# First expert layer of a four-layer tower: three float32r products of split operands for each float32 product

## What is computed

```python
logits = xf @ gate_w + gate_b
probs = jax.nn.softmax(logits, axis=-1)
gates, expert_idx = jax.lax.top_k(probs, K)          # K = 2 of E = 8
h = jax.nn.relu(jnp.einsum('nc,ech->neh', xf, w1) + b1)      # 256 -> 512
expert_out = jnp.einsum('neh,ehc->nec', h, w2) + b2          # 512 -> 256
...
out = jnp.einsum('ne,nec->nc', weights, expert_out)
return out.reshape(b, t, c)
```

## Time and profile before

| | |
|---|---|
| time, median of 3 runs | 1462.86 us (1462.44 to 1463.99) |
| the profiled execution | 1469.06 us, its span 1467.1 us |
| mean granted TensorE clock | 0.907 of full |
| TensorE busy | 1262.5 us (86% of the span) |
| VectorE busy | 956.9 us (65%) |
| GpSimd busy | 712.7 us (49%) |
| ScalarE busy | 528.6 us (36%) |
| first mixture, first to last product | 531.7 to 826.9 us |
| its tiles | 71 |

### The profile page before, as it was taken

The page is one execution under the profiler, slowest core; times in us unless marked ns, Lnnn a source line. Parts: engine busy times, 40 slices in busy tenths (PEclk is TensorE's granted clock), DMA queues, the critical chain, the costliest instruction groups (busy, mean ns, idle before and its releaser), DMA issues. The chain is left out here.

```text
span 1467.1 us, 23655 instructions
## 1 busy us (share of the span) xinstructions
PE 1262.5 (86%) x6856; PEld 891.6 (61%) x6856; DVE 956.9 (65%) x2759; ACT 528.6 (36%) x999; POOL 712.7 (49%) x912
## 2 busy tenths in 40 slices
PE   1358989989999759999999658899995899999997
PEld 0245656656666436666666447777774567667675
DVE  6657989988887455555555578999985444444443
ACT  1025545546565412222222266666652111111111
POOL 6664286282222244445555246666663454544543
PEclk9869989989999769999999868887887899999999
DMA  6266646546874513211211242321000821101000
GB/s 175 49 103 111 116 79 133 84 84 141 168 149 108 200 47 107 72 63 62 65 60 53 80 143 94 103 90 48 22 16 30 295 98 32 33 29 32 27 18 12
DMA packets 88714, 125.79 MB, mean 86 GB/s; under 512 B 17728, under 2 KB 71630, under 8 KB 87632
## 3 DMA queue, kind: packets, MB, share of 16 engines
q1 hardware_dynamic: 68800, 84.61, 25.2%
q0 software_dynamic: 16416, 38.46, 8.4%
q10 hardware_dynamic: 3376, 1.22, 0.4%
HBM read 70.71 MB, written 31.01 MB: 69 GB/s over the span
## 5 line engine op out<-in xcount | busy, mean ns | idle before, releaser
L1064 DVE TENSOR_REDUCE top_a_a<-s_bank 128x4 f32<-128x1024 f32 x128 | 156.2, 1220 | 60.0 <-PE s_bank L704 54.9
L883 ACT ACTIVATE prob_a<-s_bank 128x1024 f32<-128x1024 f32 x128 | 130.6, 1020 | 42.1 <-PE s_bank L725 39.5
L2025 PE MATMUL ebank<-w,exT 128*128 x312 | 142.7, 601 | 0.7 <-ACT exT L2071 0.7
L2036 PE MATMUL ebank<-w,ehT 128*128 x624 | 141.2, 379 | 0.9 <-ACT ehT L2079 0.9
L1582 PE MATMUL mbank<-w2T_m,fhT_m 128*128 128x256 f32 x512 | 140.6, 437 | 0.0
L615 POOL DMA_INDIRECT rows_d<-h_a,row_i_a x64 | 64.6, 1009 | 152.9 <-DVE row_i_a L1149 138.2
L1262 PE MATMUL ebank<-w,exT 128*128 x284 | 135.5, 600 | 0.6 <-ACT exT L1309 0.6
L1274 PE MATMUL ebank<-w,ehT 128*128 x568 | 134.5, 380 | 0.8 <-ACT ehT L1315 0.8
L1219 POOL DMA_INDIRECT ex<-rows_d,tile_row x71 | 72.3, 1019 | 123.8 <-DVE ey L1347 108.7
L1582 PEld LDWEIGHTS mbank<-w2T_m,fhT_m 128*128 128x128 f32 x512 | 117.2, 229 | 22.3
L2036 PEld LDWEIGHTS ebank<-w,ehT 128*128 128x128 f32 x624 | 115.6, 190 | 15.7 <-issue 1.6
(11 more groups left out here) (350 smaller groups left out, 2696.3 us busy)
## 6 DMA issues: line engine op xcount, KB each, us to landing
w<-in_L_ffn_W SPq DMA_DIRECT2D x16, 1024.0 KB, 10.3
qs_a<-parts_q_a SPq DMA_DIRECT2D x96, 128.0 KB, 4.4
ks_a<-parts_k_a SPq DMA_DIRECT2D x96, 128.0 KB, 4.6
w<-in_L_ffn_w SPq DMA_DIRECT2D x16, 512.0 KB, 5.9
image_a<-in_x SPq DMA_DIRECT2D x4, 1024.0 KB, 8.3
ya_m<-y_d SPq DMA_DIRECT2D x16, 256.0 KB, 2.8
yb_m<-y_d SPq DMA_DIRECT2D x16, 256.0 KB, 3.1
b<-in_L_ffn_b SPq DMA_DIRECT2D x8, 512.0 KB, 9.4
```

What stands on the lines that cost most here:

```text
L883: nc.scalar.activation(prob[:, j % 4].rearrange("p g t s -> p (g t s)"), s2_bank[:].rearrange("p g s -> p (g s)"), ACT.Exp, scale=HD ** -0 ...
L1064: nc.vector.tensor_reduce(top[:, j].rearrange("p g t -> p (g t)"), s1_bank[:].rearrange("p g (t s) -> p (g t) s", t=TPI), axis=AX, op=ALU. ...
L2025: last = nc.tensor.matmul(bank[1 + n % 2][:], xT[j % 2][:, ch, :], w[:, bass.ds(e, 1), at:at + 512].rearrange("p a f -> p (a f)"), start=c ...
L2036: last = nc.tensor.matmul(bank[4 + j % 2][:, 0:D], hT[j % 2][:, f, :], w[:, bass.ds(e, 1), at:at + D].rearrange("p a d -> p (a d)"), start ...
```

## The change

It touches `experts`, and the SBUF layout of its neighbours.

- Each weight and each stationary operand is split into a float32r part (rounded) and a low part (the remainder, float32r too). Each float32 product becomes three float32r products: high by high, high by low, low by high (`three`).
- Operands: ScalarE's copies to `xT` and `hT` round to float32r; VectorE subtracts for the low parts, `xl` and `hl`.
- Weights: for expert 0 ScalarE copies two halves to `wl`, VectorE subtracts (between the two halves of `maps`), ScalarE writes the rounded weights back into `w`. For experts 1 to 7 this goes in 28 pieces of 512: ScalarE `near`, GpSimd `low_of`, ScalarE `far`, one piece per tile. TensorE waits for `split_ok` of the tile's expert, with a value computed from the register.
- The second product runs two tiles behind instead of one, and hT has three buffers instead of two.
- The scaling of x into y moves from VectorE to ScalarE (`scaled`).
- The low weights lie in the upper half of the large zone; the fixed weights of `middle` move behind the biases, and tiles of `attention` and `middle` change places. TensorE no longer waits for all weights at the start of the stage.

```diff
@@ tower
+        low0 = zone0["high"]("w0_low", [P, E, 2 * F0 + F0 // P * D], F32R)
         zone_m = zones("_m")
-        sb = zone_m["high"]
+        sb = zone_m["above"]
...
@@ maps
-    def maps(first_done, all_done):
+    def maps(first_done, all_done, between=None):
         common()
         build(0, EARLY)
         c.eng.sem_inc(first_done, 1)
+        if between:
+            between()
         build(EARLY, count)
...
@@ experts
-    xT = [sb(f"exT{u}", [P, 2, P]) for u in range(2)]
+    HTR = 3
+    xT, xTl = ([sb(f"{n}{u}", [P, 2, P], F32R) for u in range(2)] for n in ("exT", "exTl"))
...
-    hT = [sb(f"ehT{u}", [P, FC, P]) for u in range(2)]
+    hT, hTl = ([sb(f"{n}{u}", [P, FC, P], F32R) for u in range(HTR)] for n in ("ehT", "ehTl"))
+    PIECE = 512
+    PIECES = [(e, at) for e in range(1, E) for at in range(0, 2 * width + D * FC, PIECE)]
+    PER = (2 * width + D * FC) // PIECE
...
+    def rounded(e, at, n):
+        return w[:, e, at:at + n].bitcast(F32R)
+
+    def three(pe, to, high, low, e, at, n, first, last):
+        whole = w[:, bass.ds(e, 1), at:at + n].rearrange("p a f -> p (a f)").bitcast(F32R)
+        rest = wl[:, bass.ds(e, 1), at:at + n].rearrange("p a f -> p (a f)")
+        nc.tensor.matmul(to, high, whole, start=first, stop=False)
+        nc.tensor.matmul(to, high, rest, start=False, stop=False)
+        return nc.tensor.matmul(to, low, whole, start=False, stop=last)
...
@@ gpsimd
+            c.run(nc.gpsimd.memset(nought[:], 0.0))
             pool.wait_ge(c.sem, c.n)
+            pool.sem_inc(nought_ok, 1)
...
                 if j >= XR:
                     pool.wait_ge(xT_ps, j - XR + 1)
-                    pool.wait_ge(own_ok, j - XR + 1)
+                    pool.wait_ge(scaled_ok, j - XR + 1)
...
+            def low_of(n):
+                e, at = PIECES[n]
+                pool.wait_ge(near_ok, n + 1)
+                nc.gpsimd.tensor_tensor(wl[:, e, at:at + PIECE], w[:, e, at:at + PIECE], wl[:, e, at:at + PIECE].bitcast(F32), ALU.subtract)\
+                    .then_inc(low_ok, 1)
+
             for j in range(count + XR + 1):
                 if j < count:
                     load(j)
                 if j >= XR + 1:
                     send(j - XR - 1)
+                if 2 <= j < 2 + len(PIECES):
+                    low_of(j - 2)
...
@@ tensor
-            for e in range(E):
-                pe.wait_ge(w_in[e], 32)
...
                 e = number[j]
-                pe.wait_ge(xT_ok, j + 1)
+                pe.wait_ge(split_ok, e + 1)
+                pe.wait_ge(xl_ok, j + 1)
...
                 for ch in range(2):
-                    last = nc.tensor.matmul(bank[1 + j % 2][:], xT[j % 2][:, ch, :],
-                                            w[:, bass.ds(e, 1), width * ch:width * (ch + 1)].rearrange("p a f -> p (a f)"),
-                                            start=ch == 0, stop=ch == 1)
+                    last = three(pe, bank[1 + j % 2][:], xT[j % 2][:, ch, :], xTl[j % 2][:, ch, :], e, width * ch, width, ch == 0, ch == 1)
...
                 for f in range(FC):
...
+                    last = three(pe, bank[4 + j % 2][:, 0:D], hT[j % HTR][:, f, :], hTl[j % HTR][:, f, :], e, 2 * width + D * f, D, f == 0, f == FC - 1)
...
-            for j in range(count + 1):
+            for j in range(count + 2):
                 if j < count:
                     g1(j)
                 if j + 1 < count:
                     expert_of(j + 1)
                     x2(j + 1)
-                if j >= 1:
-                    g2(j - 1)
+                if j >= 2:
+                    g2(j - 2)
                 if j < count:
                     th(j)
...
@@ scalar
+            def scaled(j):
+                u = j % YR
+                act.wait_ge(own_ok, j + 1)
+                nc.scalar.activation(y[u][:], x[j % XR][:, 0:D], ACT.Identity, bias=nought[:, 0:1], scale=own[u][:, 2:3]).then_inc(scaled_ok, 1)
+
+            def near(n):
+                e, at = PIECES[n]
+                if n % PER == 0:
+                    act.wait_ge(w_in[e], 32)
+                nc.scalar.activation(wl[:, e, at:at + PIECE], w[:, e, at:at + PIECE], ACT.Copy).then_inc(near_ok, 1)
+
+            def far(n):
+                e, at = PIECES[n]
+                act.wait_ge(low_ok, n + 1)
+                nc.scalar.activation(rounded(e, at, PIECE), w[:, e, at:at + PIECE], ACT.Copy).then_inc(far_ok, 1)
+                if n % PER == PER - 1:
+                    act.wait_ge(far_ok, n + 1)
+                    act.sem_inc(split_ok, 1)
+
+            act.wait_ge(w_in[0], 32)
+            half = PER * PIECE // 2
+            for at in (0, half):
+                nc.scalar.activation(wl[:, 0, at:at + half], w[:, 0, at:at + half], ACT.Copy).then_inc(near0_ok, 1)
+            for k, at in enumerate((0, half)):
+                act.wait_ge(low0_ok, k + 1)
+                nc.scalar.activation(rounded(0, at, half), w[:, 0, at:at + half], ACT.Copy).then_inc(far0_ok, 1)
+            act.wait_ge(far0_ok, 2)
+            act.sem_inc(split_ok, 1)
...
+            near(0)
+            near(1)
             x2(0)
             for j in range(count):
                 if j + 1 < count:
                     x2(j + 1)
                 th(j)
+                scaled(j)
+                if j + 2 < len(PIECES):
+                    near(j + 2)
+                if 1 <= j < 1 + len(PIECES):
+                    far(j - 1)
...
@@ vector
-            maps(maps_ok, all_maps)
+            def low_of_first():
+                half = PER * PIECE // 2
+                for k, at in enumerate((0, half)):
+                    dve.wait_ge(near0_ok, k + 1)
+                    nc.vector.tensor_tensor(wl[:, 0, at:at + half], w[:, 0, at:at + half], wl[:, 0, at:at + half].bitcast(F32), ALU.subtract)\
+                        .then_inc(low0_ok, 1)
+
+            maps(maps_ok, all_maps, low_of_first)
...
-                c.run(nc.vector.tensor_tensor(sent_to[u][:], own[u][:, 1:2], outside[:, j:j + 1], ALU.max))
-                nc.vector.tensor_scalar(y[u][:], tail[:, 0:D], own[u][:, 2:3], None, ALU.mult).then_inc(own_ok, 1)
+                nc.vector.tensor_tensor(sent_to[u][:], own[u][:, 1:2], outside[:, j:j + 1], ALU.max).then_inc(own_ok, 1)
...
+            def xl(j):
+                dve.wait_ge(xT_ok, j + 1)
+                nc.vector.tensor_tensor(xTl[j % 2][:].rearrange("p c s -> p (c s)"), bank[3 * (j % 2)][:, 0:2 * P],
+                                        xT[j % 2][:].rearrange("p c s -> p (c s)").bitcast(F32), ALU.subtract).then_inc(xl_ok, 1)
+
+            def hl(j):
+                dve.wait_ge(hT_ok, j + 1)
+                nc.vector.scalar_tensor_tensor(out=hTl[j % HTR][:].rearrange("p c s -> p (c s)"), in0=bank[6 + j % 2][:], scalar=0.0,
+                                               in1=hT[j % HTR][:].rearrange("p c s -> p (c s)").bitcast(F32), op0=ALU.max, op1=ALU.subtract)\
+                    .then_inc(hl_ok, 1)
...
-            for j in range(count + 1):
+            xl(0)
+            for j in range(count + 2):
                 if j < count:
                     g1(j)
+                if j + 1 < count:
+                    xl(j + 1)
+                if j < count:
                     owner(j)
-                if j >= 1:
-                    g2(j - 1)
+                if j >= 2:
+                    g2(j - 2)
+                if j < count:
+                    hl(j)
...
```

More of the change, by code:

```diff
@@ L116, in zones @@
                 "bias": Space(nc, bias, BIAS_BYTES, stage), "rest": Space(nc, rest, fixed - rest, stage),
-                "open": Space(nc, bias, fixed - bias, stage), "free": Space(nc, bias + BIAS_BYTES // 4, fixed - bias - BIAS_BYTES // 4, stage)}
+                "open": Space(nc, bias, fixed - bias, stage),
+                "above": Space(nc, bias + 4 * E * (F0 + D), BIAS_BYTES - 4 * E * (F0 + D), stage)}
     with ctx:
@@ L182, in tower @@
                              lane, tile_no, ones8, sends0, minus_half)
-            experts(nc, block, s, ctx, used, zone0, weights0, bias0, load_fixed, rows0_d, y0_d, cnt, ident, iota8, lane, tile_no, ones8)
+            experts(nc, block, s, ctx, used, zone0, weights0, low0, bias0, load_fixed, rows0_d, y0_d, cnt, ident, iota8, lane, tile_no, ones8)
             ctx0.close()
@@ L266, in attention @@
         sb = zone["high"]
-        h1 = [sb(f"h1_{u}", [P, TPI, ROW0]) for u in range(2)]
-        row_i = [sb(f"row_i{u}", [P, TPI, 2], I32) for u in range(2)]
         prob = sb("prob", [P, 4, 2, TPI, SEQ])
@@ L274, in attention @@
         res = sb("res", [P, TPI, D])
+        h1 = [sb(f"h1_{u}", [P, TPI, ROW0]) for u in range(2)]
+        row_i = [sb(f"row_i{u}", [P, TPI, 2], I32) for u in range(2)]
         sb = zone["open"]
@@ L1158, in attention, with experts @@
     return sem.all
-def experts(nc, block, s, ctx, used, zone, w, b, load_fixed, rows_d, y_d, cnt, ident, iota8, lane, tile_no, ones8):
```

(32 more changed lines are left out.)

2 lines of the change are left out of this document (1 added, 1 removed).

## The result

The changed kernel took 1453.31 us (median of 6 runs, 1450.18 to 1456.67) beside 1463.07 us (6 runs) for the kernel before: a ratio of 0.9915, with a 95% interval from 0.9888 to 0.9941. It is faster by about 10 us, where 35 were forecast. The profiled execution has a span of 1450.1 us, 17.0 less than that of before.

What follows compares the result with a forecast made beforehand. GpSimd was to bound the first 28 tiles at 3.85 us, then TensorE with its sequencer at 3.5: 10.5 us gained by tile 29, 24.6 over the last 41 tiles, tail nothing; 1462.86 - 35.1 = 1427.7 us, range 1412 to 1446.

Steps and rivals of the forecast that it cites:

- GpSimd, the bound of the first 28 tiles: First expert layer: GpSimd's load, send and added subtraction set the pace at 3.85 us per tile, ends 3.5 and 4.1.
- port rival: low_of holds chosen, sent_to or ey on VectorE in 28 tiles, up to 1.0 us each: 28 us, 1456; chance 0.07.
- GpSimd's sum: GpSimd's iteration in the first 28 tiles: 1.02 + 0.31 + 1.02 + 0.02 + 1.26 + 0.20 = 3.83, taken as 3.85 us.
- TensorE at 3.50: Expert tiles where nothing else binds: array 3.36 and sequencer 3.45 to 3.5, taken as 3.5 us against 4.10 before.
- The sequencer's term: TensorE's address steps for products with weights chosen by expert: 18 per tile at 0.114, 2.05 us.
- Its rival (1491): Sequencer: each of 18 address steps costs 0.17 us instead of 0.114, 4.5 us per tile, 28 us lost; chance 0.07.
- the clock (1490): Small idle times lower TensorE's clock, 6.7 us per tile at half clock; 20 such tiles lose 27 us; chance 0.05.
- The start: Before tile 0: splitting expert 0's weights delays the first product from 531.70 to near 532.6, a 0.9 us loss.
- VectorE's chain: VectorE's steps per expert tile: 3.3 us in sum, fitting under 3.5 with 0.2 to spare.
- Tail: From tile 70's first product to the stage's end: nothing gained, 7.6 us as before.
- tile 0 to 2: Stretch between the first products of tiles 0 and 2: 7.4 us forecast, 9.3 before.
- the layout: The moved SBUF tiles were to cost nothing.

Runs made afterwards that it cites:

- e4: Changed kernel with GpSimd's subtraction for experts 1 to 7 left out, its signal kept: 1422.26 us.
- e12: Changed kernel with three GpSimd fills of 360 columns, reading nothing from SBUF, in place of each subtraction: 1446.85 us (1 run).
- e6: Changed kernel with GpSimd's subtraction issued once VectorE's ey is finished, ahead of the send instead of behind it: 1434.26 us (4 runs).
- e5: Changed kernel with the low weights always read from expert 0 at a fixed address, dropping six register steps per tile: 1449.72 us.
- e7: Changed kernel with the low parts of experts 1 to 7 made by VectorE behind hl, none by GpSimd: 1426.77 us (1 run).
- e11: Same kernel as e7 (low parts on VectorE instead of GpSimd), timed with more runs: 1427.38 us (5 runs), ratio 0.9736 to the kernel before.
- e3: Changed kernel with GpSimd's subtraction covering 256 of the 512 columns of each piece of experts 1 to 7: 1427.75 us.
- e1: Changed kernel with VectorE's chosen, own and sent_to moved to the head of its turn, before g1: 1478.1 us (4 runs).

## Why the prediction was wrong

**The step that failed** is in "GpSimd, the bound of the first 28 tiles", and in the sentence that put the port rival aside: "with the load as pacemaker those VectorE steps end about 0.5 us before low_of begins". The load is no pacemaker. The send in front of `low_of` waits for VectorE's `ey`, 1.0 us in every tile, so the phase of `low_of` is set by VectorE's own chain, and 1.45 us behind `ey` that chain comes to `chosen`. I had worked out the length of GpSimd's iteration and then taken its phase for free. Price: 121.3 us for 27 tiles where 101.3 were forecast, 20.0 us of the 20.3 by which the stage missed. e4 and e12 show the cause (no reading subtraction, no hit), e6 shows that the phase alone is worth 17.0 us of it (its 27 tiles take 104.3).

**The port rival was right**, with 0.07. Its form holds: a hit in nearly every tile, about 1.5 us on one step, of which the slack of VectorE and GpSimd hides half. The loss against my 3.85 is 0.70 us per tile, not 1.0. Its time of 1456 lies 3 us above the measured one, which is partly chance: of the 25.6 us above my forecast only 20.3 come from this stage. The rows that spoke for it were on the table, though the step held there (line 1109) reads one SBUF tensor and not two, so that they did not show its form. What should have weighed more is the count: VectorE has three steps with two SBUF operands in every tile, in a chain with 0.2 us to spare, and GpSimd's subtraction covers more than a quarter of it (1.30 of 4.55 us). For the rival to fail, the two engines would have had to keep a phase that nothing enforces.

**GpSimd's sum was right** as a length: 1.02 + 0.31 + 1.02 + 0.03 + 1.30 + 0.16 = 3.84 from the rows of after, and e6 runs at 3.87.

**TensorE at 3.50 was right by compensation.** The measured 3.48 is 6 x 0.235 + 12 x 0.118 + 6 x 0.11 = 1.41 + 1.42 + 0.66 = 3.49, with the spacings of the products just shown. I had taken the lower bound, 0.216, for a product of 512 columns, where twice the float32r row would have been right. The sequencer's term, 2.05 us for 18 steps, was too large: 12 steps, and e5 shows that six fewer change nothing. (The sequencer's whole sum, moreover, is 3.37 to 3.47 by the terms given, not 3.45 to 3.5.) So the term mis-sized downward was made up for by a bound that does not exist. Its rival (1491) and the clock (1490) did not appear; the clock is 1.00 in both windows.

**The start** cost 2.1 us and not 0.9. Of the miss, 1.0 comes with the subtractions once more: one of the last map steps of VectorE meets the first `low_of`.

```profile
526.86 1.66 DVE L1402 TENSOR_SCALAR tile_sum<-tile_sum 128x71 f32<-128x71 f32 x1
```

This step takes 0.30 us in e4, e7 and e11 and 0.29 in e12, which have no subtraction on GpSimd and start 1.0 us earlier, 0.45 in e3 with half of one, and 1.66 in the changed kernel and its other variants. So the subtraction holds it, although it reads one SBUF tensor, like the step of line 1109 in rows 9; the theory of two operands does not cover it, and which steps with one operand are held was not tried.

**VectorE's chain** was summed to 3.3 us and is 3.02 (e11: 3.62 with a step of 0.60). With the larger figure a subtraction on VectorE looked too dear; it is the best place.

**Tail, tile 0 to 2, and the layout** came as forecast (7.6; 7.5 for 7.4; nothing). The tail's terms in the prediction add up to 6.4 and not 6.5, which changes nothing, since the rest was left to the sequencer.

**Between stage and time** 5 us stay open. The stage gained 14.8 us in the two profiles and the medians differ by 9.8. Attention took from 511 to 525 us in the profiles of these kernels, which compute the same there, and `middle` from 302.8 to 306.4, with nothing in the change to explain either; I have one profile of each kernel, too few to divide the rest.

## What to carry to other kernels

Before elementwise work is put on GpSimd beside a busy VectorE, list the VectorE steps with two SBUF operands (here one with a single operand was held too) and ask which wait sets the phase of GpSimd's instruction; if a VectorE step releases it, the two are locked to each other, and the same collision comes in every iteration. Put the reading GpSimd instruction where VectorE works from PSUM, or give the work to VectorE if it is twice as fast there. Equal sums on the engines say nothing of phases.

## What was not expected of the hardware

- The port is held before `low_of`'s record begins. In the changed kernel `chosen`, issued at 612.36, would have ended at 612.58 while `low_of`'s record begins at 612.77; in e1 `sent_to` would have ended 0.59 us before the record. In the same run `chosen` ended 0.65 us before a record, and was free:

```profile
613.63 0.23 DVE L1412 SCALAR_TENSOR_TENSOR chosen<-ex,tile_sum 128x6 f32<-128x6 f32 x1
```

```profile
613.47 1.02 POOL L1247 DMA_INDIRECT y_d<-ey,sent_to  x1 [1.42 <-ACT ey L1345]
614.51 1.28 POOL L1254 TENSOR_TENSOR w_low<-w,w_low 128x512 fp32r<-128x512 f32 x1
```

  Here `chosen` runs inside the record of the send, so the send does not hold the port from its start; with subtractions of 512 columns the hold begins some 0.6 us before the record behind the send. With 256 columns (e3) it is not one stretch: a `chosen` issued 0.4 us before the record, as in the changed kernel, was released 0.05 us behind the record's beginning, and six of them, issued 0.10 to 0.18 us before it, took at most 0.02 us more than alone. What separates the two is open. The Trainium skill, "Perfetto Trace Analysis", section "GPSIMD Engine Instruction", warns that the span of a GpSimd instruction in a profile is unreliable. If the hold begins with the instruction, these pairs give the error here as at least 0.59 us at its start. With the fills of e12 behind the same send nothing was held. What happens in those 0.6 us was not looked into further.
- The hit goes past other steps: `own`, a reduction with one SBUF operand, ran in 0.16 us wherever it stood, beside `low_of`'s record in 19 tiles of e3, and steps with one operand in PSUM kept their lengths beside every `low_of`.
- Float32r products with full 128-row weights, loaded anew each time, run 0.118 us apart for 256 columns and 0.23 to 0.24 for 512, at full clock: 0.55 of one float32 pass, of which each float32 product takes two. So three of them cost 0.82 of the float32 product that they replace.
